# A layer norm, a recurrent gate network and ALiBi attention on eight cores: another order of loads, of the ramp and of the last gate steps

## The chip, the cores and the metric

The kernel runs on the 8 cores of one Trainium2 chip. Each core works on one batch element of its own, and the cores exchange nothing. The metric is the device time of the slowest core in microseconds (us). A profile shows one execution on its slowest core.

## What is computed

For x of 4096 tokens by 1024 features (float32), per batch element:

```
xn = layernorm(x)
s  = attention(xn)      # 16 heads of 64, keys and queries exchanged, ALiBi bias, softmax
g  = silu(net(xn))      # three cycles, below
x  = x + s * g

gf = sigmoid(global_net(mean over tokens of xn))
out = xn
three times:
    tf  = sigmoid(gelu(gelu(gelu(out @ w1 + b1) @ w2 + b2) @ w3 + b3) @ w4 + b4)   # 1024, 512, 256, 1
    out = out + coupling(gf, tf) * twist(out)   # one number per token; twist permutes four quarters of the features
```

## The kernel before

**Engines and queues.** TensorE (PE) does the matmuls, VectorE (DVE) the norms, sums and copies, ScalarE (ACT) GELU, tanh, exp and some copies, GpSimd (POOL) the inverse square roots and all weight DMAs (they cast float32 to bf16), SyncE (SP) the other DMAs. Each engine runs its own list of instructions in order, written out by hand (`pe_program`, `act_program`, `dve_program`, `gp_program`, `sp_program`), and they wait for each other by semaphores. A waiting instruction holds everything behind it on its engine.

**Front.** Tokens come in 32 tiles of 128 (512 KB each), six buffers deep: tile t waits for the norm of tile t - 6. VectorE makes mean and variance (`stats(s)`, two tiles a pair), GpSimd turns a pair's variance into r = (var + eps)^-0.5 and nmr = -mean * r in four steps (L424 to L430), VectorE writes XN = x * r + nmr in bf16 (`norm(s)`, L1083). In VectorE's list `norm(s)` stands behind `stats(s + 1)`. PE transposes a tile (L483), ScalarE copies it into XB (L779), which holds all of xn transposed. Behind every fourth tile PE makes token sums for the global net. From tile 4 on each tile is followed by one item of the list EARLY (30 items, table SPREAD; the last three stand behind tile 31): layer 1 of blocks 0 to 2, 256 tokens each, cycle 1, with their layers 2 and 3. GpSimd issues the seven weight DMAs of both nets once tile 3 has landed (L412 to L418): W1 2048 KB as bf16, W2 1024, W3 256, W4 64, GW1 1024, GW2 256, GW3 64.

**Network.** A block is 256 tokens, 16 blocks in all (E11 to E15 are the last). Layer 1 is linear, so it is computed once for xn (U, `uv_unit(e, 0, i)`) and once for the twisted xn (V, `uv_unit(e, 1, i)`), in four units each; W1N is W1 negated, for the twist's signs. The pre-activations of cycles 2 and 3 are then sums U + c V and a U + b V on VectorE (`pre2`, `pre3`) with factors c, a, b per token that come from the cycle before (`couple1`, `couple2`, `couple3`). A cycle is: 8 GELUs (`gelu_u` or `gelu_pre`), `layer2` (32 matmuls), `gelu2`, `layer3`, `gelu3`, `layer4`, `tanh_z`, a coupling. The loop over p runs cycle 1 of block p, cycle 2 of block p - 2 and cycle 3 of block p - 3 beside each other. P_ORD and Z_ORD number the passes through the shared PSUM banks. `cab` holds what the coupling takes from the global net; no coupling can run before it.

**Gate.** When a block's three cycles are through (`gate_scalars`), its two chunks of 128 tokens are loaded again (XF), scaled on ScalarE (`scale_x`, L858 and L859), twisted and added on VectorE (`add_twist`, L1194 and L1196), passed through tanh (`tanh_y`, L865), multiplied (`gate`, L1203) and stored to g_s in HBM. Below, "chunk 14" and "chunk 15" mean the two chunks of block E14 and of E15.

**Attention.** Heads go in 8 pairs. Each pair needs projections in units of 512 tokens, 4 pieces of matmuls each: K (copied to KT), V (times the ALiBi weights, to VB) and Q (to QT). The class Plan makes the order: `groups` are up to four score blocks of 128 keys by 256 queries, one exp of up to 128 x 1024 each (1024 groups); a `job` is a pair and 256 queries (the first jobs have 14 groups). `build()` goes in rounds r: scores of groups 2r and 2r + 1 ("S"), products with V of groups 2r - 3 and 2r - 2 ("AV"), then pieces of later units ("W") as their due round, `window(u)`, asks. PE's list is P.pe. VectorE's is P.dve: W copies a unit, O copies a job's sums out of PSUM, N divides, multiplies by g, adds x; these are put in by a running estimate of when they are ready. The first n_early = 17 units (K, V and Q0 of the first pair) are made before the exps in banks 0 and 1, later ones in bank 7. SyncE loads g and x for each job (GS, XS, four buffers) and stores its result.

Of the kernel before, what the change touches and what calls it, by code (L numbers as in the profile page):

```python
# [41 lines left out]
E_LAST = NE - 1  # L42

class Plan:

# [99 lines left out]
def build_program():  # L147
# [160 lines left out]
    Z_ORD = []  # L308
    for p in range(1, NE - 1):
        if p - 3 >= 0:  # L310
            P_ORD.append((p - 3, 3))
# [39 lines left out]
    def sp_program():  # L351
        SY.dma_start(out=identb[:], in_=identb_h[:]).then_inc(sConst, 16)
        SY.dma_start(out=biases[:], in_=bias_h[:]).then_inc(sConst, 16)
        for t in range(NT):
# [1107 lines left out]
```

## Time and profile before

| | |
|---|---|
| median of 3 runs | 1543.62 us (1542.3 to 1544.22) |
| the profiled execution, its own time | 1534.47 us |
| its span on the slowest core | 1532.9 us (others 1528.3 to 1532.9) |
| PE busy | 1378.9 us (90%) |
| ACT busy | 1332.8 us (87%) |
| DVE busy | 791.6 us (52%) |
| mean granted TensorE clock | 0.98 of full speed |

The span runs from the first to the last instruction of a core; the profiled execution is 1.57 us longer than it and 9.15 us shorter than the median of the runs. Busy shares are means over stages that are bound by different things, so the stages are to be read one by one. Times in the rows are from the span's start.

### The profile page before, as it was taken

The numbers are of one execution on the slowest core, as the hardware profiler recorded it, in microseconds if no ns is written. First come the engines' busy times: TensorE is split into PE (matmuls) and PEld (weight loads), VectorE is DVE, ScalarE is ACT, GpSimd is POOL, SyncE is SP. The second block draws the span as 40 slices with busy tenths as digits, with TensorE's granted clock in tenths as the row PEclk, the third lists the DMA queues.
The fourth block names the chain that finished last, engine by engine and source line by source line (L and its number), as shares of the span: only waits on it lengthen the run. The fifth ranks groups of instructions, "written<-read, shape, count | busy, mean of one in ns | idle before, by whom it ended". The sixth has DMA issues, their size and how long they took to land.

```text
span 1532.9 us, 49645 instructions; the slowest of 8 cores (1528.3 to 1532.9 us)
## 1 busy us (share of the span) xinstructions
PE 1378.9 (90%) x18394; PEld 940.1 (61%) x18394; DVE 791.6 (52%) x1863; ACT 1332.8 (87%) x2009; POOL 49.9 (3%) x104
## 2 busy tenths in 40 slices
PE   1696799999999995999999999999999999999997
PEld 1585688888888863555755444565554444655554
DVE  2774687887878893222222333333333434434666
ACT  1355698988988874999999999999999999999998
POOL 2331000000000000000000000000000000000000
PEclk9998899999999997999999999999999999999999
DMA  8851013122121116311112112113321212222333
GB/s 177 226 163 42 26 57 111 56 73 94 57 103 65 56 56 152 91 33 33 34 47 57 43 44 64 44 43 64 78 61 54 64 53 57 71 64 73 111 106 113
DMA packets 122391, 115.58 MB, mean 75 GB/s; under 512 B 8368, under 2 KB 106928, under 8 KB 121776
## 3 DMA queue, kind: packets, MB, share of 16 engines
q1 hardware_dynamic: 118848, 101.26, 21.2%
q0 software_dynamic: 3312, 11.14, 4.6%
q8 instruction: 157, 2.57, 0.7%
q14 instruction: 74, 0.61, 0.1%
HBM read 89.96 MB, written 33.55 MB: 81 GB/s over the span
## 4 chain that ended last, share of the span: by engine, by line
PE 77%; DVE 7%; issue 5%; DMA 4%; ACT 4%; DVEq 2%; POOL 0%; SPq 0%; ACTq 0%; POOLq 0%
PE PS L747 20%; PE PS L765 18%; PE PS L513 14%; PE PS L529 11%; PE PS L613 9%; ACT PB L877 3%; DMA XT<-x 3%; PE PS L608 3%; PE PS L541 3%; DVE ACC L1375 3%; DMA XF<-x 1%; DVE SST L1393 1%; PE PS L483 1%; DVE QT L1229 0%; PE PS L554 0%
## 5 line engine op out<-in xcount | busy, mean ns | idle before, releaser
L877 ACT ACTIVATE PB<-PS 128x1024 bf16<-128x1024 f32 (+2 forms) x1088 | 906.8, 1037 | 9.6 <-PE PS L747 8.3
L747 PE MATMUL PS<-QT,KT 64*128 64x256 bf16 x3888 | 373.3, 273 | 39.4 <-ACT PB L877 21.3
L765 PEld LDWEIGHTS PS<-VB,PB 128*128 128x128 bf16 x7776 | 274.8, 97 | 167.6 <-issue 165.9
L765 PE MATMUL PS<-VB,PB 128*128 128x66 bf16 x7776 | 344.7, 194 | 24.8 <-DVE ACC L1375 23.4
L747 PEld LDWEIGHTS PS<-QT,KT 64*128 64x128 bf16 x3888 | 147.1, 94 | 265.8 <-issue 239.7
L513 PE MATMUL PS<-XB,W 128*128 128x256 bf16 x1536 | 207.8, 276 | 0.0
L529 PE MATMUL PS<-H,W 128*128 128x256 bf16 x1536 | 181.9, 276 | 10.4 <-ACT H L802 9.6
L1375 DVE COPY ACC<-PS 128x264 f32<-128x264 f32 x128 | 55.4, 432 | 228.6 <-PE PS L765 228.3
L529 PEld LDWEIGHTS PS<-H,W 128*128 128x128 bf16 x1536 | 150.1, 99 | 32.8 <-issue 14.6
L613 PE MATMUL PS<-XB,WQ 128*128 128x512 bf16 x512 | 154.4, 385 | 10.7 <-DVE VB L1225 7.8
L513 PEld LDWEIGHTS PS<-XB,W 128*128 128x128 bf16 x1536 | 150.2, 99 | 18.5
L820 ACT ACTIVATE H<-PS,biases_s 128x256 bf16<-128x256 f32 x192 | 80.7, 474 | 56.0 <-PE PS L529 54.4
L1393 DVE SCALAR_TENSOR_TENSOR SST<-ACC,den,GS 128x64 f32<-128x64 f32 x512 | 111.7, 280 | 12.5 <-issue 2.6
L1229 DVE CAST QT<-PS 128x512 bf16<-128x512 f32 x64 | 44.2, 691 | 142.7 <-PE PS L613 142.6
L608 PE MATMUL PS<-WKV,XB 128*128 128x128 bf16 x1152 | 83.0, 219 | 1.4 <-DVE KT L1229 1.3
L791 ACT ACTIVATE H<-U,biases_s 128x256 bf16<-128x256 f32 x128 | 59.1, 503 | 27.2 <-DVE U L1097 27.2
L613 PE MATMUL PS<-XB,WKV 128*128 128x512 bf16 x288 | 81.2, 378 | 0.5 <-DVE KT L1229 0.5
L513 PE MATMUL PS<-XB,W1N 128*128 128x256 bf16 x512 | 77.5, 274 | 0.0
L1229 DVE CAST KT<-PS 128x512 bf16<-128x512 f32 x36 | 24.9, 690 | 87.3 <-PE PS L613 87.1
L483 PE MATMUL PS<-identb_s,XN 128*128 128x128 bf16 x256 | 22.9, 244 | 51.3 <-DVE XN L1083 42.0
L608 PEld LDWEIGHTS PS<-WKV,XB 128*128 128x128 bf16 x1152 | 66.1, 97 | 2.3 <-issue 1.8
L802 ACT ACTIVATE H<-PRE,biases_s 128x256 bf16<-128x256 f32 x128 | 61.2, 502 | 4.1 <-DVE PRE L1126 4.1
(98 smaller groups left out, 1177.6 us busy)
## 6 DMA issues: line engine op xcount, KB each, us to landing
XT<-x SPq DMA_DIRECT2D x32, 512.0 KB, 5.4
XF<-x SPq DMA_DIRECT2D x32, 512.0 KB, 5.5
g_s<-TY SPq DMA_DIRECT2D x32, 512.0 KB, 3.0
GS<-g_s SPq DMA_DIRECT2D x128, 128.0 KB, 2.5
XS<-x SPq DMA_DIRECT2D x128, 128.0 KB, 2.4
out<-SST SPq DMA_DIRECT2D x128, 128.0 KB, 1.8
WKV<-wkv POOLq DMA_DIRECT2D x8, 512.0 KB, 7.6
W<-w POOLq DMA_DIRECT2D x1, 2048.0 KB, 17.9
```

Of the source, the lines that this page charges most:

```text
L513: x = TE.matmul(bank[:, q * TE_:(q + 1) * TE_], w, XB[:, src * S + e * TE_:src * S + (e + 1) * TE_], start=(f == 0), stop=(f == NF - 1))
L529: x = TE.matmul(bank[:, q * TE_:(q + 1) * TE_], W2[:, f * 512 + f2 * 128:f * 512 + (f2 + 1) * 128], H1[cyc - 1][:, f * TE_:(f + 1) * TE_], ...
L608: x = TE.matmul(bank[:, piece * 128:(piece + 1) * 128], XB[:, f * S + nt * 128:f * S + (nt + 1) * 128], w[:, f, :], start=(f == 0), stop=( ...
L613: x = TE.matmul(bank, w[:, f, :], XB[:, f * S + c * 512:f * S + (c + 1) * 512], start=(f == 0), stop=(f == NF - 1))
L747: x = TE.matmul(BANK[2 * (g % 3) + b % 2][:, (b // 2) * 256:(b // 2 + 1) * 256], KT[i][hh * 64:(hh + 1) * 64, (nt - KT0[i]) * 128:(nt - KT ...
L765: x = TE.matmul(BANK[6][:, (2 * hh + j) * VW:(2 * hh + j + 1) * VW], PB[g % NPB][:, col_of(b) + j * 128:col_of(b) + (j + 1) * 128], vbv[i] ...
L802: SE.activation(out=H1[cyc - 1][:, f * TE_:(f + 1) * TE_], in_=src[:, q * TE_:(q + 1) * TE_], func=AF.Gelu, bias=b1c[:, f:f + 1]).then_inc ...
L820: k = SE.activation(out=H2[n % 2][:, f * TE_:(f + 1) * TE_], in_=BANK[3 + i][:, q * TE_:(q + 1) * TE_], func=AF.Gelu, bias=b2c[:, f:f + 1])
L877: x = SE.activation(out=dst[:, k, t], in_=src[:, k, t], func=AF.Exp, bias=-MARGIN, scale=1.0 / 32.0)
L1229: VE.tensor_copy(out=dst[:, c0 * 512:(c0 + 1) * 512], in_=bank).then_inc(vU, 1)
L1375: VE.tensor_copy(out=ACC[n % NACC][:], in_=BANK[6][:, 0:4 * VW]).then_inc(vO, 1)
L1393: VE.scalar_tensor_tensor(out=SST[k][:, c0:c0 + 64], in0=acc[:, b, 0:64], scalar=rd[:, b:b + 1], in1=GS[k][:, c0:c0 + 64], op0=AOP.mult, o ...
```

## The change

1. **Front.** W1 leaves first, in two parts (six eighths, two eighths), without waiting for a tile; SyncE holds tile 3 and all behind it until the first part has landed. W2 to W4 are issued behind GpSimd's second pair, the global net's weights behind its seventh. EARLY's items stand behind tiles 2 to 31, one each. VectorE adds eps itself (a drain and a TENSOR_SCALAR of 128 x 2 in `stats`); GpSimd's power takes the variance as it is, and `norm` waits for it alone (XN = (x - mean) * r, the mean from VectorE's own tile). GpSimd still makes nmr, for the gate.
2. **Ramp.** The passes p = 1 to 4 of the loop are written out in another order on PE, ACT and DVE: units of block 3 stand between the cycles of blocks 0 and 1. The loop begins at p = 5.
3. **Into the exps.** Before the exps stand 12 units (eight K, Q0, three V); the V units 3 to 7 follow among the first rounds, one in each of rounds 0 to 4. The gate steps of chunk 14 move in among the exps (scaling before groups 8 and 9, tanh before 14 and 15), those of chunk 15 from groups 2 to 5 to groups 28, 29, 36 and 37. VectorE has them as ("G", 0) to ("G", 3) in P.dve, which now begins with the copies of V3 to V7, then G0, O0, the copy of Q1, G1, N0, Q2, O1, Q3, G2, N1, Q4, G3. SyncE stores chunk 14 and loads chunk 15 behind the first eight loads of GS and XS, and stores chunk 15 behind the second store of a result.

```diff
+NV0 = 3
+GATE_AT = (10, 16, 30, 39)
...
-        first, later = self.pair_units(0), []
-        self.n_early = len(first) - (NC - 1)
-        later += first[self.n_early:]
+        units = self.pair_units(0)
+        first = [u for u in units if u[0] == "K"] + [("Q", 0, 0)] + [u for u in units if u[0] == "V"][:NV0]
+        later = [u for u in units if u not in first]
+        self.n_early = len(first)
...
+        if kind == "V" and i == 0:
+            g = min(g for g in range(self.first[(0, 0)], self.last[(0, 0)] + 1)
+                    if any(nt // 4 == c for _, nt, _ in self.groups[g][2]))
+            return 0, (g + 3) // 2 + 1
...
+        gates = [(through[g], 14, ("G", k)) for k, g in enumerate(GATE_AT)]
         for when, cost, op in urgent:
+            while gates and gates[0][0] < when:
+                free = max(free, gates[0][0]) + gates[0][1]
+                self.dve.append(gates.pop(0)[2])
...
-    SPREAD = [EARLY[k - 4:k - 3] if 4 <= k < NT - 1 else EARLY[NT - 5:] if k == NT - 1 else [] for k in range(NT)]
+    SPREAD = [EARLY[k - 2:k - 1] if k >= 2 else [] for k in range(NT)]
...
         for t in range(NT):
+            if t == 3:
+                SY.wait_ge(sW1[0], 16)
...
-        for e in range(NE):
+        def load_x(e):
...
+        def store_g(e):
...
+        for e in range(NE - 2):
+            load_x(e)
+            store_g(e)
+        load_x(NE - 2)
...
         for n in range(NST):
             load(n)
+        store_g(NE - 2)
+        load_x(NE - 1)
         for n in range(NP * NQ):
             SY.wait_ge(vF, n + 1)
             SY.dma_start(out=rows(out_h, n), in_=slot(SST, n)).then_inc(sSO[n % NST], 16)
+            if n == 1:
+                store_g(NE - 1)
...
-        GP.wait_ge(sX[3], 16)
-        GP.dma_start(out=W1[:], in_=w1_h[:]).then_inc(sW1, 16)
-        GP.dma_start(out=W2[:], in_=w2_h[:]).then_inc(sWF, 16)
...
+        GP.dma_start(out=W1[:, 0:6 * D], in_=w1_h[:, 0:6 * D]).then_inc(sW1[0], 16)
+        GP.dma_start(out=W1[:, 6 * D:], in_=w1_h[:, 6 * D:]).then_inc(sW1[1], 16)
         for s in range(NT // 2):
             GP.wait_ge(vStat, s + 1)
...
-            GP.tensor_scalar(out=r, in0=mv[:, :, 1], scalar1=EPS, scalar2=None, op0=AOP.add).then_inc(gVar, 1)
-            GP.wait_ge(gVar, s + 1)
-            GP.tensor_tensor(out=r, in0=r, in1=minus_half[:], op=AOP.pow).then_inc(gRstd, 1)
+            GP.tensor_tensor(out=r, in0=mv[:, :, 1], in1=minus_half[:], op=AOP.pow).then_inc(gRstd, 1)
...
+            if s == 1:
+                GP.dma_start(out=W2[:], in_=w2_h[:]).then_inc(sWF, 16)
...
+            if s == 6:
+                GP.dma_start(out=GW1[:], in_=gw1_h[:]).then_inc(sGW, 16)
...
-        for p in range(1, NE - 1):
+        layer4(0, 1)
+        uv_unit(3, 0, 0)
+        layer4(1, 1)
+        uv_unit(3, 0, 1)
+        uv_unit(3, 0, 2)
+        layer2(0, 2)
+        layer3(0, 2)
+        layer4(0, 2)
+        layer4(2, 1)
+        layer2(1, 2)
+        layer3(1, 2)
+        layer4(1, 2)
+        layer2(0, 3)
+        uv_unit(3, 0, 3)
+        layer3(0, 3)
+        uv_unit(3, 1, 0)
+        layer4(0, 3)
...
+        layer3(4, 1)
+        for p in range(5, NE - 1):
...
-        project(12)
...
-        project(16)
...
-                    TE.wait_ge(vU, P.uidx[("Q", i, c // 2)] + 1)
+                    TE.wait_ge(vU, max(P.uidx[("Q", i, c // 2)] + 1, P.n_early))
...
+                if (i, c) == (0, 0):
+                    TE.wait_ge(vU, max(P.uidx[("V", 0, nt // 4)] for _, nt, _ in blocks) + 1)
...
-        scale_x(2 * E14)
-        scale_x(2 * E14 + 1)
-        tanh_y(2 * E14)
-        tanh_y(2 * E14 + 1)
         for g in range(NG):
-            if g in (2, 3):
-                scale_x(2 * E_LAST + g - 2)
-            if g in (4, 5):
-                tanh_y(2 * E_LAST + g - 4)
+            if g in (8, 9):
+                scale_x(2 * E14 + g - 8)
+            if g in (14, 15):
+                tanh_y(2 * E14 + g - 14)
+            if g in (28, 29):
+                scale_x(2 * E15 + g - 28)
+            if g in (36, 37):
+                tanh_y(2 * E15 + g - 36)
...
-                x = VE.bn_aggr(mv[:, 2 * j:2 * j + 2], st[:, 12 * j:12 * j + 12])
-            x.then_inc(vStat, 1)
+                VE.bn_aggr(mv[:, 2 * j:2 * j + 2], st[:, 12 * j:12 * j + 12])
+            VE.drain()
+            VE.tensor_scalar(out=mv[:, 1:4:2], in0=mv[:, 1:4:2], scalar1=EPS, scalar2=None,
+                             op0=AOP.add).then_inc(vStat, 1)
...
-            VE.wait_ge(gNmr, s + 1)
+            VE.wait_ge(gRstd, s + 1)
...
+                c0 = 4 * (s % NMV) + 2 * (li % 2)
+                VE.tensor_scalar(out=XN[li % NXN][:], in0=XT[li % NXT][:], scalar1=mvs[:, c0:c0 + 1],
+                                 scalar2=rcol[:, li:li + 1], op0=AOP.subtract, op1=AOP.mult).then_inc(vNorm, 1)
...
+            elif op == ("G", 0):
+                add_twist(2 * E14)
+                add_twist(2 * E14 + 1)
+                gate_scalars(E15)
+            elif op == ("G", 1):
+                gate(2 * E14)
+                gate(2 * E14 + 1)
+            elif op == ("G", 2):
+                add_twist(2 * E15)
+                add_twist(2 * E15 + 1)
+            elif op == ("G", 3):
+                gate(2 * E15)
+                gate(2 * E15 + 1)
```

## Rows read from the trace of the kernel before

**Rows 1.** Stretches: us, busy us of each engine (instructions), granted clock, DMA share, GB/s.
```profile
20.00:45.00 25.00, 4.72 (x64) 4.19 (x64) 9.15 (x18) 5.14 (x5) 4.78 (x11) 1.00 1.01 191
...
141.50:183.10 41.60, 26.22 (x218) 18.64 (x216) 23.94 (x28) 20.44 (x53) 1.18 (x2) 0.75 0.22 58
183.10:210.90 27.80, 27.80 (x267) 24.94 (x265) 22.76 (x36) 24.27 (x56) 0.00 (x0) 1.00 0.22 77
...
580.00:614.00 34.00, 16.48 (x178) 9.86 (x175) 12.10 (x24) 15.41 (x18) 0.00 (x0) 0.70 0.56 150
...
650.00:700.00 50.00, 48.19 (x707) 25.72 (x706) 13.00 (x39) 50.00 (x60) 0.00 (x0) 1.00 0.12 34
```

**Rows 2.** Timeline, 14 to 142 us: start, us, engine, line, operation [idle before, releaser].
```profile
14.75 0.66 POOL L412 DMA_DIRECT2D W<-w  x1 [13.27 <-DMA XT<-x]
...
20.55 1.53 DVE L1083 TENSOR_SCALAR XN<-XT,rcol,nmr 128x1024 bf16<-128x1024 f32 x2 [4.66 <-POOL nmr L430]
...
38.14 0.69 DVE L1068 BATCH_NORM_STATS2 stat<-XT 128x6 f32<-128x512 f32 x1 [11.93 <-DMA XT<-x]
...
45.92 3.62 PE L513 MATMUL PS<-XB,W 128*128 128x256 bf16 x16
...
64.46 1.01 PE L483 MATMUL PS<-identb_s,XN 128*128 128x128 bf16 x8 [3.40 <-ACT XB L779]
...
141.93 0.94 PE L568 MATMUL PS<-gctb,GW 128*128 128x1 bf16 x32
```

**Rows 3.** The page, DMA issues: engine, count, KB each, us to landing.
```profile
W<-w POOLq DMA_DIRECT2D x1, 2048.0 KB, 17.9
```

**Rows 4.** DMA packets of 12 to 14 us (tiles alone) and 20 to 26 us (W1 alone).
```profile
DMA packets 204, 0.74 MB, mean 371 GB/s; under 512 B 23, under 2 KB 23, under 8 KB 204
...
DMA packets 63, 1.03 MB, mean 172 GB/s; under 512 B 0, under 2 KB 0, under 8 KB 0
```

**Rows 5.** Timeline of the ramp, VectorE and TensorE.
```profile
145.79 0.15 DVE L1260 TENSOR_SCALAR cab<-cab 128x1 f32<-128x1 f32 x1
...
172.86 5.56 PE L529 MATMUL PS<-H,W 128*128 128x256 bf16 x28 [2.00 <-ACT H L802]
...
199.08 3.66 PE L513 MATMUL PS<-XB,W 128*128 128x256 bf16 x32
202.57 3.66 PE L529 MATMUL PS<-H,W 128*128 128x256 bf16 x32
...
226.89 3.66 PE L513 MATMUL PS<-XB,W 128*128 128x256 bf16 x32
```

**Rows 6.** The ramp as one stretch, columns as in rows 1.
```profile
145.90:226.90 81.00, 67.44 (x581) 55.77 (x582) 61.09 (x87) 58.19 (x136) 0.86 (x2) 0.89 0.19 56
```

**Rows 7.** Timeline before the exps, TensorE, then ScalarE.
```profile
577.03 9.09 PE L608 MATMUL PS<-WKV,XB 128*128 128x128 bf16 x160
593.25 3.57 PE L613 MATMUL PS<-XB,WQ 128*128 128x512 bf16 x8 [7.13 <-DVE VB L1225]
...
592.20 0.81 ACT L858 ACTIVATE TY<-XF,fin 128x512 f32<-128x512 f32 x1 [1.34 <-DMA XF<-x]
...
598.27 1.28 ACT L877 ACT_TABLE_LOAD   x1 [1.88 <-PE PS L747]
...
606.85 0.81 ACT L858 ACTIVATE TY<-XF,fin 128x512 f32<-128x512 f32 x1 [5.34 <-DMA XF<-x]
...
608.27 1.00 ACT L877 ACTIVATE PB<-PS 128x1024 bf16<-128x1024 f32 x1
...
611.49 1.04 ACT L865 ACTIVATE XF<-TY 128x1024 f32<-128x1024 f32 x1
...
614.29 26.45 ACT L877 ACTIVATE PB<-PS 128x1024 bf16<-128x1024 f32 x31
```

**Rows 8.** Chain that ended last: start, us, what.
```profile
577.11 14.96 DMA XF<-x
...
600.41 6.30 DMA XF<-x
```

More of the change, by code:

```diff
@@ L78, in __init__ @@
         later.sort(key=lambda u: (self.window(u)[1], u[1], "KVQ".index(u[0]), u[2]))
-        self.units = first[:self.n_early] + later
+        self.units = first + later
         self.uidx = {u: r for r, u in enumerate(self.units)}
@@ L263, in build_program @@
     sX = [sem(f"sX{i}") for i in range(NXT)]
-    sW1, sWF, sGW, sWT = sem("sW1"), sem("sWF"), sem("sGW"), sem("sWT")
+    sW1 = [sem(f"sW1{i}") for i in range(2)]
+    sWF, sGW, sWT = sem("sWF"), sem("sGW"), sem("sWT")
     sWKV = [sem(f"sWKV{i}") for i in range(NKV)]
@@ L625, in early_item @@
                 if (e, v, i) == (0, 0, 0):
-                    TE.wait_ge(sW1, 16)
+                    for k in range(2):
+                        TE.wait_ge(sW1[k], 16)
                 if (e, v, i) == (0, 1, 0):
@@ L649, in pe_program @@
         TE.wait_ge(aT, NT)
-        for p in range(1, NE - 1):
+        layer4(0, 1)
[15 more added lines that the diff above has]
+        layer4(0, 3)
+        uv_unit(3, 1, 1)
+        uv_unit(3, 1, 2)
+        layer2(3, 1)
+        uv_unit(3, 1, 3)
+        uv_unit(4, 0, 0)
+        layer3(3, 1)
+        uv_unit(4, 0, 1)
+        layer2(1, 3)
+        layer4(3, 1)
+        layer2(2, 2)
+        layer3(1, 3)
+        uv_unit(4, 0, 2)
+        layer4(1, 3)
+        layer3(2, 2)
+        uv_unit(4, 0, 3)
+        layer4(2, 2)
+        uv_unit(4, 1, 0)
+        uv_unit(4, 1, 1)
+        layer2(4, 1)
+        uv_unit(4, 1, 2)
+        uv_unit(4, 1, 3)
+        layer3(4, 1)
+        for p in range(5, NE - 1):
             A, F, B, C, _ = runs(p)
@@ L760, in pe_program @@
                         TE.wait_ge(gWhl, i + 1)
+                if (i, c) == (0, 0):
+                    TE.wait_ge(vU, max(P.uidx[("V", 0, nt // 4)] for _, nt, _ in blocks) + 1)
+                if P.first[(i, c)] == g:
                     if g > 0:
@@ L1257, in dve_program @@
         VE.wait_ge(aGF, 3)
+        VE.wait_ge(gNmr, NT // 2)
         VE.scalar_tensor_tensor(out=cab[:, 2:3], in0=thg[:], scalar=0.7, in1=arc, op0=AOP.mult, op1=AOP.mult)
@@ L1261, in dve_program @@
         VE.drain()
-        for p in range(1, NE - 1):
+        couple1(0)
+        pre2(0, 0)
+        pre2(0, 1)
+        couple1(1)
+        pre2(1, 0)
+        pre2(1, 1)
+        couple2(0)
+        pre3(0, 0)
+        pre3(0, 1)
+        couple1(2)
+        pre2(2, 0)
+        empty_u(3, 0)
+        empty_u(3, 1)
+        pre2(2, 1)
+        empty_u(3, 2)
+        couple2(1)
+        empty_u(3, 3)
+        pre3_products(1, 0)
+        couple3(0)
+        gate_scalars(0)
+        pre3_sum(1, 0)
+        pre3(1, 1)
+        add_twist(2 * 0)
+        add_twist(2 * 0 + 1)
+        empty_u(4, 0)
+        empty_u(4, 1)
+        gate(2 * 0)
+        gate(2 * 0 + 1)
+        couple1(3)
+        pre2(3, 0)
+        pre2(3, 1)
+        empty_u(4, 2)
+        couple3(1)
+        gate_scalars(1)
+        empty_u(4, 3)
+        couple2(2)
+        pre3(2, 0)
+        pre3(2, 1)
+        for p in range(5, NE - 1):
             A, F, B, C, Dg = runs(p)
```

130 lines of the change are left out of this document (89 added, 41 removed).

## The prediction, made before the result was known

> **What bounds the kernel now.** I read the page first, then a table of stretches, then the timeline of the three places in which TensorE is not full. Four stages follow one another. From 0 to 142 us the input is normalized and transposed, with the first three 256-token blocks of the coupling network put between the tiles; from 142 to 227 us the network's pipeline fills; from 227 us it runs in periods; then come the first projections, and from 614 us the exps of the attention. In a period PE is busy 27.80 of 27.80 us, and from 650 us on ACT is busy 50.00 of 50.00 us [rows 1]: the change touches neither, and a stage shifted as a whole keeps its length. PE idles in the front (4.7 us busy of 20 to 45 us), in the ramp (26.2 of 41.6 us, granted clock 0.75) and before the exps (16.5 of 34 us, clock 0.70) [rows 1]. All the change can give lies there.
>
> **Part 1, the front.** Before, the weights (seven casting DMAs) go out behind the fourth tile, from 14.75 us on and 0.66 us each, and GpSimd's first steps for a norm stand behind them, so that the first norm waits 4.66 us for nmr; the seventh tile, asked for at 22 us, lands among the weights and stops VectorE for 11.93 us until 38.14. The first unit of layer 1 runs at 45.92 us, at half clock (3.62 us), and the transposes of tile 8 at 64.46 us [rows 2]. W1 takes 17.9 us from issue to landing [rows 3]; alone on the engines it moves 172 GB/s (counted in bf16), while tiles alone move 371 GB/s [rows 4].
> After, W1 leaves at about 1.5 us, six eighths of it (1.57 MB) first; SyncE holds tile 3 until they are there. My estimate: 1.57 MB at 172 GB/s is 9.1 us, tiles 0 to 2 (1.57 MB) at 371 are 4.2 us, and the engines start near 4 to 7 us, so tile 3 is asked for at 17 to 20 us (the bound from above is the row of W1: 1.5 + 17.9 = 19.4) and lands some 4 us later. Stats of pair 1 end near 24.5; norm 0 follows at once, since the pow of pair 0 is long done; then stats 2 and norm 1 (4 x 0.69 + 1.5 = 4.2 us [rows 2]) give the first unit at 29 to 30 us, now behind tile 2 instead of tile 4. Tiles 6 and 7 come at about 30, tiles 8 and 9 against W2 to W4 (1.35 MB, 7.8 us of the engines). I put tile 6, whose step now holds the item that tile 8 had, at 45 us against 64.46. Ends: 41 if the tiles don't feel the weights, 55 if they take the 16 us that tile 6 took. The DMAs of W2 to W4 now stand before pair 2 on GpSimd's queue, those of the global net before pair 7; three issues take 2 us, and a pair's result is not needed until a pair later: no cost.
> What follows to the global net took 141.93 - 64.46 = 77.5 us [rows 2]. It holds two transposes more between items (0.9 us), the last step no longer holds three items, and VectorE has a drain and a tiny TENSOR_SCALAR more in each pair: 0.23 us by the nearest pair of rows (the drain and 0.15 us of L1260) [rows 5], 13 pairs, 3.0 us, of which half lies where PE and not VectorE is late. GpSimd's shorter way (pow alone) is worth nothing here, since norm(s) runs behind stats(s+1): only the first norm ever waited for POOL. With up to 1 us for the global net's weights, now loaded in the fifties: 77.5 + 0.9 + 1.5 + 1 = 80.9. The global net starts at 126, **gain 16 us**, ends 6 and 20.
>
> A rule of the Trainium skill bears on this (DMA: Bandwidth & Descriptors, Queues, rings and completion order): each DMA engine goes round robin between its queues, packet by packet. By it the big packets of W1 would slow tiles 0 to 2 as well, against the order that the change wants; the trace agrees as far as tile 6 shows it. By that rule the first unit comes at about 31 instead of 29.5, inside the ends above.
>
> **Part 2, the ramp.** From cab known (145.9) to the first unit of block 5 (226.9) are 81.0 us [rows 5]. Unit pairs and layer 2 start 3.49 us apart, and a period (block 4's to block 5's unit) is 27.81 us [rows 5]. The work of PE between is two periods, 55.6, and one layer 2, a layer 3 and three layers 4 of block 0 and 1, 5.3: 61 us, so 20 us are waits and half clock. The busy times of the stretch are 67.4, 61.1 and 58.2 us (PE, DVE, ACT) [rows 6]: no order ends it under about 65 us with VectorE's drains, and that is the upper end of the gain, 16.
> I walked the new lists by hand with these durations, on the clock of before. Units 3,0,0 to 3,0,2 (5.3 us) run while PE waits for pre2 of block 0, so layer 2 of (0,2) runs at full clock and ends at 156.7. GELUs of (0,2), coupling, pre3 and the GELUs of (0,3) follow; nothing shortens these. Layer 2 of (0,3) ends at 174.8, against 172.86 + 5.56 = 178.4 [rows 5], with 6 us more of the list done. From there PE's list holds 13 units, 4 layers 2, 5 layers 3 and 4 layers 4: 22.8 + 14.0 + 4.4 + 1.0 = 42.2 us, and I find no wait in it, since the list never asks for a block within 5 us of the GELUs that feed it. Block 5 starts at 217.3 instead of 226.9. VectorE's list ends its last pre3 at 215.6 and ACT's its last GELU at 217.9, so all three are level and a late one has no cover; the later start of periods is then the same as before. **Gain 9.5 us**, ends 3 and 13.
>
> **Part 3, the way into the exps.** Before, PE makes five V units in 9.09 us from 577.03 and then waits 7.13 us for VectorE, which stands at the twist of chunk 14, behind ACT and a load of 14.96 us; exps 0 and 1 run from 599.6, exp 2 waits for the next load (5.34 us), and only from exp 5 at 614.29 do they run end to end, 31 in 26.45 us, 0.853 each [rows 7, 8]. Counted back, that is a start at 614.29 - 5 x 0.853 = 610.0 with all gate work done.
> After, Q0 takes the ninth place, three V units stay, and scores start when V2 is copied. PE has layer 4 of the last block done and V2 begun at 577.0, so + 1.8 + 0.7 for the copy: 579.9; the table load of 1.28 us [rows 7] puts exp 0 at 582. Rounds 0 to 4 (two groups each) carry a whole V unit: 9.09 / 5 = 1.8 us, beside 2 x 0.58 for scores and products (48.2 us of PE for 60 exps between 650 and 700, less half a piece each [rows 1]): 2.9 us, where ACT needs 1.7. Five rounds end at 594. ACT meanwhile has the two scalings of chunk 14 before exps 8 and 9, 1.42 us each (606.85 to 608.27), the second of which waits for its load until 592.2, as before; exp 10 starts at 594.5. From there ACT sets the pace. Left are two tanh (1.04 us long, 0.95 apart by the 0.1 that scalings overlap: 0.81 long, 0.71 apart) and chunk 15's two scalings and two tanh: 1.9 + 4.7 = 6.6 us. Counted back: 594.5 - 8.5 + 6.6 = 592.6, **gain 17.4 us**, ends 8 and 20.
> What is queued behind the moved steps: VectorE's two gates of chunk 14 stand behind O0 and Q1's copy and run at about 602 to 604, SyncE's store of chunk 14 stands behind the eight loads of GS and XS (over by 590) and goes at 604, the load of chunk 15 at 606. At 6.30 us it lands at 612 [rows 8], when exp 28 is due (594.5 + 1.9 + 18 x 0.853 = 611.8): no slack. The store of chunk 15 stands behind the second store of out and ahead of the loads for job 5, which are needed 40 us later; GpSimd's weight columns and jobs 14 and 15 that wait for it are hundreds of us away.
>
> A rule of the Trainium skill speaks against this part (ScalarE: Activation LUTs, Table sets: the hidden batching unit): activations should be batched by table set. Eight returns to another set, with a load each way as in the row, would cost 16 x 1.28 = 20 us and eat the gain. In the trace chunk 15's scaling and tanh already stand between exps without a load, so I give it nothing; the page's own list has tanh in the set of exp.
>
> **Sum.** 16 + 9.5 + 17.4 = 42.9 us. The profiled execution took 1534.47 us and would take 1491.6; the runs' median is 1543.62, 9.15 above it, and I keep that distance: 1500.7, given as 1501.
>
> **Rivals.** *A, the tiles starve:* each tile takes 16 us while any weight is loading; the item of tile 8 comes at 55. For it speaks the row of 11.93 us, against it that before 4.6 MB of weights stood ahead and now 1.35. Front 6: 1511. *B, chunk 15's load is long:* 14.96 us like chunk 14's instead of 6.30 holds exp 28 by 8.7 us: 1509. For it: the eight loads of GS and XS; against: they and the WQ loads are over by then. *C, PE is the bound among the exps:* it is 96% busy there (48.2 of 50 us [rows 1]), and the five V units (9.1 us) then come on top: 1510. *D, slower:* the hand order of the ramp crosses a chain. From cab to layer 2 of (0,3) are 27.1 us for two cycles of one block [rows 5], 13.5 a cycle; an engine that stands at the head of its list for a result of a later cycle costs that each time. The ramp's gain and four such waits, 9.5 + 54, give 1564; it decides from the fourth on (42.9 / 13.5 = 3.2). My walk found none. *E, no change:* the waits come back elsewhere: A (10), B (8.7), C (9.1) and a ramp without gain (9.5) together leave 5.6, and one wait more of that size leaves 1543.
>
> **Chances.** Forecast 0.61, A 0.12, B 0.11, C 0.08, better than the ends' middle by over 10 us 0.04, D 0.02, E 0.02. About 0.2% (3 us) is what a measurement of this kernel can tell from no change. Faster 0.96, same 0.02, slower 0.02. The range takes in A, B and C alone, and from the ends of the three parts (42.9 + 13, - 17) 1488 to 1518.
>
> **What would show it.** Right: first layer 1 unit near 30 us and the global net near 126; block 5's first unit near 201.4; exp 0 near 556.5 (582 less 25.5) and exp 10 near 569; ACT full from there; PE's clock near 1.00 in the ramp. Wrong: VectorE waiting over 5 us for tiles behind pair 3; ACT idle at L858 among the exps; a wait of PE over 3 us in the ramp; exps apart by more than 0.853 after the fifth round.

## The result, and the profile after

The changed kernel takes 1518.2 us (three executions from 1517.24 to 1518.20) beside 1543.92 for the kernel before: a ratio of 0.9833 (95% interval 0.9814 to 0.9853), 25.7 us faster. The forecast was 1501 with a range up to 1518. The direction was right, the size was not. The profiled execution took 1518.16 us (executions in which cores of a die ran some 40 us or more longer, at a mean clock below 0.95, are left out everywhere). The spans and mean granted clocks of its cores:

```profile
core 0: 1504.7 us, clock 0.989
core 1: 1502.2 us, clock 0.990
core 2: 1502.0 us, clock 0.987
core 3: 1504.4 us, clock 0.989
core 4: 1514.5 us, clock 0.982
core 5: 1511.6 us, clock 0.981
core 6: 1514.1 us, clock 0.981
core 7: 1516.6 us, clock 0.979
```

Before, all eight stood between 1528.3 and 1532.9 at 0.979 to 0.981. Now they fall into two groups: four gained 27 to 28 us, four only 14 to 21, at a lower clock. Core 7 sets the time; core 3 shows what the change does without that.

**The front** (timeline of core 7; start, us, engine, line, operation, idle before), to be laid beside [rows 2]:

```profile
1.89 0.67 POOL L431 DMA_DIRECT2D W<-w  x1 [0.42 <-issue]
...
19.84 0.69 DVE L1203 BATCH_NORM_STATS2 stat<-XT 128x6 f32<-128x512 f32 x1 [11.19 <-DMA XT<-x]
...
27.57 1.53 DVE L1222 TENSOR_SCALAR XN<-XT,mvs,rcol 128x1024 bf16<-128x1024 f32 x2
...
33.80 3.62 PE L533 MATMUL PS<-XB,W 128*128 128x256 bf16 x16
...
45.48 0.69 DVE L1203 BATCH_NORM_STATS2 stat<-XT 128x6 f32<-128x512 f32 x1 [3.85 <-DMA XT<-x]
...
50.94 1.01 PE L503 MATMUL PS<-identb_s,XN 128*128 128x128 bf16 x8 [4.75 <-DVE XN L1222]
...
135.99 0.94 PE L588 MATMUL PS<-gctb,GW 128*128 128x1 bf16 x32
```

VectorE gets tile 1 only at 19.84 us, after 11.19 us of waiting beside W1; it gets the ninth tile (tile 8) at 45.48, after 3.85 us more of waiting; the first unit of layer 1 runs at 33.80 (before 45.92), tile 6 is transposed at 50.94, and the global net starts at 135.99 (before 141.93).

**The network** (stretches: busy us of PE, PEld, DVE, ACT, POOL with the number of instructions, then granted clock, DMA share, GB/s; first core 7, then cores 2 and 3), to be laid beside [rows 1]:

```profile
core 7: us, PE busy (x) PEld busy (x) DVE busy (x) ACT busy (x) POOL busy (x), PEclk, DMA share, GB/s
141.50:183.10 41.60, 34.98 (x274) 27.45 (x272) 35.02 (x47) 28.70 (x69) 0.00 (x0) 0.84 0.24 52
218.00:221.00 3.00, 3.00 (x25) 2.49 (x23) 2.16 (x3) 1.96 (x4) 0.00 (x0) 0.81 0.00 0
300.00:400.00 100.00, 100.00 (x924) 88.58 (x922) 78.66 (x118) 83.53 (x190) 0.00 (x0) 0.97 0.27 85
650.00:700.00 50.00, 48.25 (x712) 25.91 (x709) 12.22 (x34) 49.91 (x61) 0.00 (x0) 1.00 0.11 31
...
core 2: us, PE busy (x) PEld busy (x) DVE busy (x) ACT busy (x) POOL busy (x), PEclk, DMA share, GB/s
141.50:183.10 41.60, 34.96 (x283) 28.02 (x281) 34.86 (x49) 30.60 (x74) 0.00 (x0) 0.88 0.11 31
...
core 3: us, PE busy (x) PEld busy (x) DVE busy (x) ACT busy (x) POOL busy (x), PEclk, DMA share, GB/s
141.50:183.10 41.60, 34.23 (x299) 27.92 (x297) 35.56 (x49) 31.61 (x76) 0.00 (x0) 0.96 0.22 57
300.00:400.00 100.00, 100.00 (x955) 89.73 (x954) 80.42 (x129) 87.47 (x200) 0.00 (x0) 1.00 0.27 83
```

The start of the ramp is fuller (35.0 us of PE in 41.6, before 26.2). Its clocks of 0.84, 0.88 and 0.96 there are the half clock alone, which core 7 shows for 12.9 of these 41.6 us, core 2 for 10.2 and core 3 for 3.4. In the periods PE is busy without a gap on cores 3 and 7, yet core 7 does 924 matmuls in 100 us where core 3 does 955. The difference is in stretches of some 5 us, from 183 us on and about one in each period, in which the granted clock is neither of the two levels of the kernel before (1.00 and 0.50 of 2.4 GHz) but 0.81. In the profile of the kernel before no core shows that value.

**The exps** (timeline of core 3):

```profile
564.74 1.28 ACT L935 ACT_TABLE_LOAD   x1 [2.88 <-PE PS L802]
566.04 3.77 ACT L935 ACTIVATE PB<-PS 128x1024 bf16<-128x1024 f32 x4
570.32 1.94 ACT L935 ACTIVATE PB<-PS 128x1024 bf16<-128x1024 f32 x2 [0.52 <-PE PS L802]
573.39 1.94 ACT L935 ACTIVATE PB<-PS 128x1024 bf16<-128x1024 f32 x2 [1.12 <-PE PS L802]
...
576.47 1.11 PE L628 MATMUL PS<-WKV,XB 128*128 128x128 bf16 x17 [1.09 <-issue]
...
578.06 1.02 ACT L935 ACTIVATE PB<-PS 128x1024 bf16<-128x1024 f32 x1 [1.33 <-PE PS L802]
...
580.39 4.59 ACT L935 ACTIVATE PB<-PS 128x1024 bf16<-128x1024 f32 x6
...
599.26 0.96 ACT L916 ACTIVATE TY<-XF,fin 128x512 f32<-128x512 f32 x1
```

Rounds are 3.07 us apart (570.32 to 573.39), the scaling of chunk 15 finds its load landed (599.26, no wait), and no second table load follows the first.

### The profile page after: what moved, and what is told of

Read it like the earlier page. It is cut to its first block, busy times and chain, and to the rows that moved or that the text cites. A ratio compares the mean times of both kernels' runs of the same rounds, so it can differ in the third digit from the quotient of the medians.

```text
span 1516.6 us, 49662 instructions; the slowest of 8 cores (1502.0 to 1516.6 us)
## 1 busy us (share of the span) xinstructions
PE 1386.6 (91%) x18394; PEld 946.6 (62%) x18394; DVE 795.5 (52%) x1879; ACT 1333.5 (88%) x2009; POOL 38.7 (3%) x89
## 4 chain that ended last, share of the span: by engine, by line
PE 79%; DVE 6%; issue 5%; ACT 4%; DMA 4%; DVEq 1%; ACTq 0%; POOL 0%; SPq 0%; POOLq 0%
PE PS L802 20%; PE PS L823 18%; PE PS L533 14%; PE PS L549 11%; PE PS L633 9%; PE PS L628 4%; ACT PB L935 3%; DMA XT<-x 3%; PE PS L561 3%; DVE ACC L1551 2%; DMA W<-w 1%; DVE SST L1569 1%; PE PS L574 1%; PE PS L503 0%; DVE QT L1368 0%
## 5 line engine op out<-in xcount | busy, mean ns | idle before, releaser
L533 PE MATMUL PS<-XB,W 128*128 128x256 bf16 x1536 | 215.8, 284 | 0.0
L533 PEld LDWEIGHTS PS<-XB,W 128*128 128x128 bf16 x1536 | 153.9, 102 | 22.3
L633 PE MATMUL PS<-XB,WQ 128*128 128x512 bf16 x512 | 151.2, 378 | 4.3 <-DVE QT L1368 2.2
L1364 DVE TENSOR_TENSOR VB<-PS,WT 128x512 bf16<-128x512 f32 x36 | 24.9, 691 | 84.4 <-PE PS L628 83.7
```

The lines of the kernel that those rows point to most:

```text
L533: x = TE.matmul(bank[:, q * TE_:(q + 1) * TE_], w, XB[:, src * S + e * TE_:src * S + (e + 1) * TE_], start=(f == 0), stop=(f == NF - 1))
L633: x = TE.matmul(bank, w[:, f, :], XB[:, f * S + c * 512:f * S + (c + 1) * 512], start=(f == 0), stop=(f == NF - 1))
```

## The experiments

The experiments ran in five groups (e to i), each on a chip of its own, here called 2 to 6; the result's chip is called 1, and the records don't tell which it is. The kernel before ran beside each group, at a median of 1536.65 to 1538.82 us. To compare parts, I cut every profiled execution at three stations that lie on the path: the global net's first matmul, block 5's first unit, the first exp. The values are means over the cores that show no 0.81, unless cores are named (us):

| kernel | chip | global net | to block 5 | to exp 0 | to the end | ratio of times, 95% interval |
|---|---|---|---|---|---|---|
| before | 1 | 139.8 | 85.2 | 373.3 | 932.7 | |
| changed, cores 0 to 3 | 1 | 135.0 | 77.0 | 354.8 | 936.5 | |
| changed, cores 4 to 7 | 1 | 136.0 | 78.3 | 363.7 | 936.2 | 0.9833 (0.9814 to 0.9853) |
| e1 changed, cores 6 and 7 | 2 | 134.2 | 77.5 | 354.8 | 935.9 | 0.9971 (0.9945 to 0.9996) |
| e2 part 1 alone | 2 | 136.2 | 86.2 | 373.2 | 932.4 | 0.9960 (0.9937 to 0.9984) |
| e3 part 2 alone | 2 | 139.6 | 78.6 | 372.9 | 932.3 | 0.9942 (0.9904 to 0.998) |
| e4 part 3 alone | 2 | 140.9 | 85.7 | 354.8 | 935.7 | 0.9883 (0.9835 to 0.9931) |
| f1 parts 1 and 3 | 3 | 135.7 | 86.0 | 354.8 | 935.3 | 0.9872 (0.9858 to 0.9886) |
| f2 softened ramp | 3 | 136.5 | 82.3 | 354.8 | 936.2 | 0.9846 (0.983 to 0.9861) |
| f3 f1, GW late | 3 | 133.6 | 86.0 | 354.8 | 935.8 | 0.9858 (0.9844 to 0.9872) |
| f4 f1, eps on POOL | 3 | 132.9 | 85.4 | 354.8 | 936.5 | 0.9859 (0.9845 to 0.9873) |
| g1 changed | 4 | 135.9 | 77.2 | 354.8 | 936.3 | 0.9816 (0.9803 to 0.9829) |
| g2 softened ramp | 4 | 136.2 | 82.4 | 354.8 | 935.7 | 0.9852 (0.9839 to 0.9865) |
| g3 two of three units | 4 | 136.0 | 77.8 | 354.8 | 935.9 | 0.9822 (0.9809 to 0.9834) |
| g4 g2, eps and GW | 4 | 130.2 | 82.6 | 354.8 | 935.5 | 0.9813 (0.98 to 0.9825) |
| h1 changed, eps and GW | 5 | 130.6 | 77.1 | 354.8 | 935.5 | 0.9788 (0.9775 to 0.9801) |
| h2 h1, W1 later | 5 | 135.1 | 77.3 | 354.8 | 935.7 | 0.9804 (0.9791 to 0.9817) |
| h3 h1, W2 later | 5 | 128.2 | 78.0 | 354.8 | 935.9 | none given |
| h4 as g4 | 5 | 132.1 | 82.5 | 354.8 | 935.7 | 0.9829 (0.9814 to 0.9843) |
| i1 as h3 | 6 | 129.1 | 77.2 | 354.8 | 934.9 | 0.9769 (0.9755 to 0.9783) |
| i2 i1, two of three units | 6 | 129.1 | 77.3 | 354.8 | 936.0 | 0.9768 (0.9754 to 0.9782) |

In one execution a core's global net lies up to 9 us from another's, and its mean over the cores is 130.2 in g4 and 132.1 in h4, which are the same kernel, so below 2 us the ratios decide. The ratio of e3 stands for its four executions without 0.81 (1528.48 to 1530.77 us); its other seven took 1552.03 to 1554.13 us, more than the kernel before.

### Which part gives what (e1 to e4)

e1 is the changed kernel as it is. e2, e3 and e4 are the kernel before with one of the three parts of the diff; to part 1 belongs one line of the change that the excerpt of its diff leaves out, so that the gate may still use nmr:

```diff
         VE.wait_ge(aGF, 3)
+        VE.wait_ge(gNmr, NT // 2)
```

> The changed kernel once more, beside the kernel before. Its profile gave 28.0 us less than before on core 3 (1532.4 to 1504.4) and 16.3 less on core 7 (1532.9 to 1516.6), where a period of the network is 28.6 us long instead of 27.8 and the granted clock is 0.93 to 0.97 in it. Theory C (the chip's clock): the lower clock of one die is there in timed executions of the kernel before as well, so the ratio stays near 0.983 and the gain near 26 us. Theory P (the plan): the change itself draws the clock down, since TensorE pauses less; then before shows both dies level in every run and the changed kernel never does.

> Part 1 alone (order of the weight DMAs, items from tile 2 on, eps on VectorE, power alone on GpSimd). Theory A (the parts add, each as its stage shows in the trace): global net at about 135 instead of 141.6, 6 to 7 us faster. Rival B (the front's gain depends on what follows it, since the old ramp starts slower behind a busier front): under 4 us or over 10.

> Part 2 alone (passes 1 to 4 in the new order). Theory A: block 5 starts 8 to 9 us sooner, 8 to 9 us faster. Rival B: under 5 us, if the ramp lives on the front's new tail.

> Part 3 alone (12 units ahead of the exps, gate of the last two blocks among them). Theory A: 13 us faster, with exps 0 to 9 about 3.1 us a round. Rival B (DMA traffic at that point decides): the same trace but another length of the loads, gain under 10 or over 16.

By the stages, part 1 gives 4 to 5 us at the global net (of which e2 loses 1 again in the ramp), part 2 gives 7 to 8, part 3 gives 18.5 - 3.0 = 15.5: together some 28, what cores 0 to 3 of the result show. By the ratios the parts are 6, 9 and 18 us, with intervals of 4 to 7 us either way that take in the values of the stages. That is near theory A for e2 and e3; e4 gives more than the 13 us expected. But e1 took 1534.63 us (median), nearly the time of before: the cores of before are level in all but one execution and those of the changed kernel in none, as theory P has it. Its spans and clocks, then stretches of core 5 and core 7:

```profile
core 0: 1530.5 us, clock 0.969
...
core 5: 1532.0 us, clock 0.969
core 6: 1504.5 us, clock 0.988
core 7: 1500.3 us, clock 0.990
...
core 5: us, PE busy (x) PEld busy (x) DVE busy (x) ACT busy (x) POOL busy (x), PEclk, DMA share, GB/s
...
200.00:300.00 100.00, 100.00 (x793) 83.02 (x792) 68.86 (x105) 73.23 (x164) 0.00 (x0) 0.81 0.21 69
...
320.00:420.00 100.00, 100.00 (x952) 89.71 (x951) 80.85 (x120) 86.05 (x196) 0.00 (x0) 1.00 0.28 86
...
core 7: us, PE busy (x) PEld busy (x) DVE busy (x) ACT busy (x) POOL busy (x), PEclk, DMA share, GB/s
200.00:300.00 100.00, 100.00 (x946) 89.68 (x945) 82.47 (x122) 86.44 (x193) 0.00 (x0) 1.00 0.20 72
```

Six cores run at 0.81 from about 148 us on, a few us into the ramp, to about 310 us, broken only by the half clock of the ramp's waits. Core 5 then does 793 matmuls where core 7 does 946, and ends some 30 us later. It comes by pairs of neighbouring cores. With the whole change all 12 otherwise undisturbed executions had one to three such pairs (mean clock near 0.967), with the ramp alone 7 of 11, with part 1 alone none of 11, with part 3 alone none of 4, with the kernel before 1 of 25. So on this chip the new order of the ramp makes it common, though it can come without it.

### Does the filled wait at the ramp's start draw it (f1, f2, g1 to g3, h4, i2)

f1 is parts 1 and 3 with the ramp of before. f2 and g2 are the whole change with three units of PE moved:

```diff
         layer4(0, 1)
-        uv_unit(3, 0, 0)
         layer4(1, 1)
-        uv_unit(3, 0, 1)
-        uv_unit(3, 0, 2)
         layer2(0, 2)
...
         layer4(1, 2)
+        uv_unit(3, 0, 0)
+        uv_unit(3, 0, 1)
+        uv_unit(3, 0, 2)
         layer2(0, 3)
```

In g3 only `uv_unit(3, 0, 2)` is moved so; g1 is the changed kernel again.

> Parts 1 and 3 of the change, with the ramp's order of before. Theory P (the denser ramp is what draws the granted clock of 0.81): no stretch of 0.81 on any core, all eight cores within 0.5% of one another, and the gain is the sum of the two parts alone, 4.8 + 15.5 = 20 us: ratio 0.987 (0.985 to 0.989), faster than the whole change on the same kind of chip (0.9971). Theory F (anything that shortens the stages ahead of the network draws it, the front as well): pairs of cores with 0.81 again, 25 to 30 us longer, ratio 0.995 or above.

> The whole change, but the three units of block 3 that filled PE's wait ahead of layer 2 of (0,2) stand behind layer 4 of (1,2). Theory H1 (it is the filling of that wait, without a pause of PE at the start of the ramp, that starts the long stretch of 0.81): none of it here; the cores lose at most 3 us of fill against the undisturbed cores of the whole change (1500 to 1504 us), so 1504 to 1507 and a ratio near 0.981. Theory H2 (the ramp as a whole is too dense, wherever its units stand): stretches of 0.81 on some cores as before, 1530 us on them, ratio 0.995 to 0.999.

> The whole change once more, beside its variants on one chip, since the runs with and without the granted clock of 0.81 so far were on different chips. Theory P (the ramp's order draws it, on any chip): some pairs of cores have stretches of 0.81 in the network stage, a mean clock of 0.97 to 0.982 and 1512 to 1534 us, the others 0.988 and 1500 to 1505 us; the slowest core sets 1518 to 1535. Theory C (only some chips do it, whatever the ramp): either all of this call's kernels show it, or none, and then the whole is at 1505 to 1508 and a ratio near 0.981.

> As before (the three units behind layer 4 of (1,2)), now on the same chip as the whole change. Theory H1 (filling PE's wait at the ramp's start draws the 0.81): no 0.81 where the whole change shows it, all cores 1507 to 1512 us. Theory C: the same cores show it as in the whole change's run. Where neither shows it, soft is 5 us slower than the whole change: 82.4 us from the global net to block 5 against 76.4.

> Two of the three units of block 3 stay in PE's wait ahead of layer 2 of (0,2), the third moves behind layer 4 of (1,2), so PE pauses there for some 1.8 us. Theory H1 as a matter of degree: between the whole change and soft, block 5 at 78 to 81 us behind the global net, and 0.81 on fewer cores than in the whole change, or none. Theory H1 as a matter of any pause: none of 0.81. Theory C: as the whole change.

f1 has the sum of its two parts by the stages (its ratio of 0.9872 is 19.7 us, forecast 20), without 0.81. f2 has none either, and it looked like a confirmation, but it ran on another chip than e1. g1, on a third, shows that the chip decides too: no core of the changed kernel has 0.81 there, and it takes 1508.25 us, ratio 0.9816. With nothing to avoid, softening costs 5.2 us of the ramp (82.4 against 77.2). TensorE's timeline of core 4, first in g1, then in g2, shows why:

```profile
146.35 0.60 PE L549 MATMUL PS<-H,W 128*128 128x256 bf16 x4
147.10 4.09 PE L549 MATMUL PS<-H,W 128*128 128x256 bf16 x28 [0.15 <-ACT H L860]
...
212.31 3.66 PE L533 MATMUL PS<-XB,W 128*128 128x256 bf16 x32
```

```profile
146.04 1.57 PE L549 MATMUL PS<-H,W 128*128 128x256 bf16 x4 [3.21 <-ACT H L860]
148.48 6.23 PE L549 MATMUL PS<-H,W 128*128 128x256 bf16 x28 [0.87 <-ACT H L860]
...
168.28 6.80 PE L533 MATMUL PS<-XB,W 128*128 128x256 bf16 x48
...
220.29 3.66 PE L533 MATMUL PS<-XB,W 128*128 128x256 bf16 x32
```

Where PE waited 3.21 us the layer 2 behind it runs mostly at half clock, 6.23 us for 28 matmuls, where after the filled wait it takes 4.09, and the three units now stand where PE has no wait for them to fill (6.80 us from 168.28 on). g3 with two of three units in the wait loses 0.6 us by the stages and 0.9 by the ratios, whose intervals overlap.

Groups h and i put the ramps side by side once more. h4 is g4's kernel, to be compared with h1, which has the full ramp; i2 is i1 with g3's edit.

> The first kernel with the softened ramp, on the same chip. Where no core shows 0.81: 5 us slower than the first kernel, 1508. Where the chip grants 0.81 to the dense ramp and theory H1 holds: all cores 1500 to 1506 us, no 0.81, and 15 to 25 us faster than the first kernel. Where H2 holds (any shorter ramp draws it): 0.81 on pairs of cores here too.

> The same with one of the three units of block 3 behind layer 4 of (1,2). Where neither shows 0.81: 0.7 us slower (0.6 us as the whole change and its variant on one chip). Where the first shows it: theory H1 as a matter of any pause, no pair of cores at 0.967 to 0.973 in any execution; as a matter of degree, fewer than in the first.

By the ratios h4 is 6.3 us slower than h1 (0.9829 against 0.9788), and i2 is level with i1. On chip 5 the kernels with the full ramp (h1 to h3) had a pair at a mean clock near 0.97 and some 22 us longer in 3 of 13 executions, the softened one in none of 3; on chip 6 neither kernel had any. These executions were not the profiled ones, so that they had 0.81 stretches is inferred from their clocks. Three against none is too few to show that the filled wait, and not the ramp as a whole, is what matters: that stays open. Shown is only that e3's edit makes the long stretches common on chip 2.

### Why the front gave 4 to 6 us of 16 (f3, f4, g4, h1 to h3, i1)

f3 issues the global net's weights later; f4 gives eps back to GpSimd but lets norm wait for the power alone, as the change does:

```diff
-            if s == 6:
+            if s == 11:
```

```diff
-            GP.tensor_tensor(out=r, in0=mv[:, :, 1], in1=minus_half[:], op=AOP.pow).then_inc(gRstd, 1)
+            GP.tensor_scalar(out=r, in0=mv[:, :, 1], scalar1=EPS, scalar2=None, op0=AOP.add).then_inc(gVar, 1)
+            GP.wait_ge(gVar, s + 1)
+            GP.tensor_tensor(out=r, in0=r, in1=minus_half[:], op=AOP.pow).then_inc(gRstd, 1)
...
-            VE.drain()
-            VE.tensor_scalar(out=mv[:, 1:4:2], in0=mv[:, 1:4:2], scalar1=EPS, scalar2=None,
-                             op0=AOP.add).then_inc(vStat, 1)
+            x.then_inc(vStat, 1)
```

> Parts 1 and 3, the three loads of the global net's weights issued behind GpSimd's pair 11 instead of 6. Theory G (these 1.3 MB starve the tiles near 62 to 80 us): VectorE's waits for tiles there (1.97 and 0.95 us) go, and the global net starts 1.5 to 3 us earlier than in the kernel with parts 1 and 3. Theory S (tiles are late from the first weights on, and stay so at the pace of VectorE and PE): under 0.7 us; or later, if the weights come too late for the global net (landing behind 125 us).

> Parts 1 and 3, eps added on GpSimd as before (one more GpSimd step ahead of the power), VectorE without its drain and TENSOR_SCALAR in stats; norm still waits for the power alone. Theory V (VectorE's addition is on the path of the front: 0.35 us a pair over 13 to 15 pairs): the global net starts 2 to 5 us earlier. Theory N (VectorE has slack, or the longer GpSimd step makes the norm wait instead): within 1 us, with a wait of VectorE for rcol at the first pair of 0.5 us or more.

> Soft, with eps added on GpSimd as in the kernel before (norm still waits for the power alone) and the loads of the global net's weights behind pair 11. Alone beside parts 1 and 3 these gave 2.8 and 2.1 us at the global net (mean of the cores). Theory A (they add up, since both free VectorE's and the tiles' path): the global net at 131 to 132.5 us, 1508 us in all, the fastest of the four. Theory B (both take away the same wait): 2.5 to 3 us in all, 1510.

> The whole change, with eps added on GpSimd again (norm waits for the power alone) and the loads of the global net's weights behind pair 11. On the softened ramp the two took 6 us off the start of the global net (136.2 to 130.2, mean of the cores) and 5.4 us off the time. Theory A (the front's gain goes through whole): 1508.3 less 5.5, about 1503, ratio 0.978, on a chip without 0.81, the fastest of all. Theory P (the dense ramp, on a chip that grants 0.81): pairs of cores 20 to 30 us longer, slower than the kernel with the softened ramp of this call.

Each gives some 2 us by the ratios, whose intervals overlap with f1's (2.1 for f3 and 2.8 for f4 at the global net), and together 6.0 on the softened ramp (0.9852 to 0.9813, 136.2 to 130.2) and 4.3 on the full one (g1's 0.9816 to h1's 0.9788, on two chips; 5.3 at the global net): they add up, within the scatter. So eps on VectorE is a loss of 2 to 3 us as made: the drain and the extra operation lie on VectorE's path (in the changed kernel norm starts 0.46 us behind the start of the aggregate, in h1 0.20), while what they spare GpSimd is hidden, since norm(s) stands behind stats(s + 1).

h2 and h3 take away the two collisions by themselves:

```diff
+        GP.wait_ge(sX[2], 16)
         GP.dma_start(out=W1[:, 0:6 * D], in_=w1_h[:, 0:6 * D]).then_inc(sW1[0], 16)
```

```diff
-            if s == 1:
+            if s == 3:
                 GP.dma_start(out=W2[:], in_=w2_h[:]).then_inc(sWF, 16)
```

> As the one before, but W1 is issued only when tile 2 has landed. Theory R (W1 and the tiles share the DMA engines packet by packet, and so tile 1 comes at 20 instead of 9 us): tiles 1 and 2 are read by 10 to 12 us, W1's first part lands 9 to 12 us after its issue near 11, tile 3 follows at 24 to 26; the first unit of layer 1 at 28 to 30 instead of 34 us, and the global net 3 to 5 us earlier. Theory S (the same bytes have to pass either way): tile 3 comes as much later as tiles 1 and 2 come earlier, and the global net moves by less than 1 us either way, or 2 us later, since the engines stand idle while W1's descriptors are made.

> As the first, but W2 to W4 behind GpSimd's pair 3 instead of 1. Theory A (rival A of the prediction: a tile takes 16 us while these weights load, which stops VectorE for 4.6 us near 45 us): the wait moves to tiles 10 and 11, which have more tiles ahead of them; the global net starts within 1.5 us of the first kernel's. Theory B (the early tiles are the ones that matter, since PE has nothing else then): the global net 3 us earlier. Theory D (W2 comes too late for the first layer 2): PE waits for W2 near 60 us, global net later.

> The kernel with W2 to W4 behind pair 3 once more: 1500 to 1502 us where no core shows 0.81, ratio 0.976 to 0.978; theory B (the early tiles matter) holds if the ratio is below 0.9778, the interval's middle of the kernel with W2 to W4 behind pair 1 less 0.1%. Theory P: on a chip that grants 0.81, some executions with a pair of cores at a mean clock of 0.967 to 0.973 and 1518 to 1527 us.

In h2 (core 3, timeline, and W1's row of its DMA issues) tile 1 does come at 9.49 us, and W1's first part, alone on the engines, lands 11.8 us after its issue instead of 16.4 in h1:

```profile
9.49 0.69 DVE L1206 BATCH_NORM_STATS2 stat<-XT 128x6 f32<-128x512 f32 x1 [1.08 <-DMA XT<-x]
...
11.22 0.66 POOL L432 DMA_DIRECT2D W<-w  x1 [9.75 <-DMA XT<-x]
...
29.43 0.69 DVE L1206 BATCH_NORM_STATS2 stat<-XT 128x6 f32<-128x512 f32 x1 [17.15 <-DMA XT<-x]
...
36.84 2.90 PE L536 MATMUL PS<-XB,W 128*128 128x256 bf16 x16
```

```profile
W<-w POOLq DMA_DIRECT2D x1, 1536.0 KB, 11.8
```

But tile 3, which waits for it, comes at 29.43 us (25.87 in h1), and norm 0 stands behind its stats: the first unit is 3.6 us later (33.27 in h1), the global net 4.5 by the mean of the cores and 2.5 by the ratios (0.9804 against 0.9788, overlapping). Theory R has the early tiles and W1's landing right and what follows wrong; theory S is right in kind, but the global net moves by more than its 2 us. So sharing was not the loss. That a first norm which does not wait for tile 3 would help is my reading of the list; no run tests it. h3 and i1 keep VectorE fed where it had nothing else. VectorE's longest wait for a tile behind the first three, core 3, in h1 and then in i1:

```profile
45.58 0.69 DVE L1205 BATCH_NORM_STATS2 stat<-XT 128x6 f32<-128x512 f32 x1 [4.45 <-DMA XT<-x]
```

```profile
52.82 0.69 DVE L1205 BATCH_NORM_STATS2 stat<-XT 128x6 f32<-128x512 f32 x1 [3.33 <-DMA XT<-x]
```

The wait moves four tiles on and shrinks, and the time falls: h3's two executions without a pair at the lower clock took 1499.97 and 1502.01 us beside 1502.45 to 1506.86 of h1's four, and i1, on another chip, has a ratio of 0.9769. Its middle is below the bound set for theory B, but the intervals of h1 and i1 overlap, so 1 to 3 us is likely and not certain. i1 and i2, 1503.23 and 1502.77 us beside 1538.82, are the fastest kernels with a ratio of their own: some 36 us below before, where the change alone gave 25.7 and 28.4.

## Why the prediction was wrong in size

The forecast had the profiled execution's span at 1532.9 - 42.9 = 1490.0 us; core 7 took 1516.6. The stations split the 26.6 us that are missing, up to rounding:

| stage, core 7 | forecast | measured | missing |
|---|---|---|---|
| global net starts | 126 | 135.99 | 10.0 |
| to block 5 (201.4 - 126) | 75.4 | 80.5 | 5.1 |
| to exp 0 (582 - 226.9) | 355.1 | 364.2 | 9.1 |
| to the end | 933.5 | 936.0 | 2.5 |

(933.5 is 1532.9 - 17.4 less 582.) The 9.15 us between the profiled execution and the median, which I kept, were gone after the change: the other executions agree with the profiled one. That is why the miss against 1501 is 17 us and not 26.6: a gap that I could not explain, and that no run explains, hid 9 us of it by luck.

**The term "gain 16 us" of the front failed.** Three of its steps were short. The first unit was put at 29.5 and came at 33.80: I gave tiles 0 to 2 their 4.2 us at 371 GB/s, as if they left before W1; they shared with it, tile 1 came at 19.84, and 17.4 us from issue to landing were near the bound from [rows 3]. Here the trace had spoken, and so had the Trainium skill (DMA: Bandwidth & Descriptors, Queues, rings and completion order), whose round robin between queues I priced at 1.5 us: it agrees, as tile 1's 19.8 us beside W1 and 9.5 in h2 without it show, but h2 also shows that without the sharing the front is no faster. The step to tile 6 was 17.1 us instead of 15.5, and from tile 6 to the global net 85.0 instead of 80.9, where VectorE's addition of eps cost 2 to 2.8 us (I took 1.5) and the global net's weights about 2 (I took 1). Rival A was half right: tile 8, asked for at 32.9 us beside W2 to W4, is read only at 45.48, but VectorE waits 3.85 us for it, where it waited 11.93 for tile 6 before. Tile 6, whose norm stands behind the stats of tiles 8 and 9, is transposed at 50.9, between the 45 of the forecast and the 55 of the rival. That GpSimd's shorter way is worth nothing here agrees with f4, which has a step more on GpSimd and is no slower. The nearest rows gave 0.23 us for drain and addition; they took 0.26 in the pair above.

**The ramp was right, without the clock.** 9.5 us forecast, 8.2 measured as the mean of cores 0 to 3, which have no 0.81 (85.2 to 77.0), and the walk missed no chain: rival D is out. These four differ: core 2 needs 79.0 us, the others 76.3 to 76.5, and core 2 alone has 17.0 us of half clock in it, where the others have 6.8. That layer 2 of (0,2) would run at full clock because the wait ahead of it is filled was right too (4.09 against 6.23 us above).

**The clock was no term of the sum at all.** The sign was "near 1.00 in the ramp"; the row has 0.84 (before 0.75), all of it half clock. Core 7 has 17.0 us of half clock in the ramp as core 2 has, and with it core 2 is 2.6 us behind cores 0, 1 and 3 (79.0 against 76.4). From 183.3 us on come the stretches of 0.81: they leave core 7 another 1.5 us behind core 2 in the ramp (80.5 against 79.0) and cost 9.4 us up to the exps (364.2 against 354.8 on core 3, which runs the same list). On chip 1 these 11 us are more than the ramp gave, on chip 2 the long stretch eats nearly all of the change. The trace of before did not show such a value, but it did show PE busy without a gap in the periods on all cores at once (28.00 of 28.00 us from 230 to 258), and a change that makes this state begin earlier and more abruptly deserved a rival. The Trainium skill has one (TensorE: Matmul & The Clock Gate, Seeing it yourself): a limiter that sets a whole die to 13/16 of full clock once three of its cores run dense matmuls. The level agrees (0.81). The rest differs: here it takes pairs of cores, for 5 us in a period or for some 160 us once, on two of six chips' profiles, and the same dense load runs at 1.00 on the others.

**The exps were right but for 2 to 3 us.** Exp 0 came 354.8 us behind block 5 on all cores at full clock, forecast 355.1. From there I had 933.5 and measured 934.9 to 936.5: rounds took 3.07 us for 2.9, and on core 3 PE paused 1.09 us between two halves of a V unit, so that exp 10 came 14.4 us (core 7) to 15.3 us (core 3) behind exp 0, forecast 12.5. Gain 15.5 of 17.4. Rival B is out (chunk 15's scaling waits for nothing), C is out (ACT 49.91 of 50 us from 650 on). On the table loads the row decides: one load at exp 0 and none at the scalings and tanhs among the exps. The 16 loads that I held against this part don't follow from the Trainium skill (ScalarE: Activation LUTs, Table sets: the hidden batching unit): its list has tanh in the set of exp and the identity, which the scalings are, in every set, and the trace agrees.

## What to carry to other kernels

Cut profiles before and after at a few stations on the path and price each stage over all cores: sums that failed by 26.6 us fell apart into four terms at once. An operation put on the engine that often sets a stage's pace costs time however small (from aggregate to norm 0.46 us a pair with drain and addition, 0.20 without, 2 to 3 us of the kernel), while what it spares an engine that nobody waits for is worth nothing. A large load that the first matmuls need may go ahead of the first tiles (h2, which held it back, was 2.5 to 4.5 us slower); later loads are better held back by a few pairs (h3 and i1, likely 1 to 3 us). Look at the first consumer's place in its queue before blaming the transfer. Before a difference between cores is put down to one level of the clock, list the stretches of each level on both.

## What the runs showed of the hardware

A granted clock of 0.81, between the two levels, in 5 us stretches in each period (cores 4 to 7 of the result) or in one from about 148 to 310 us (e1). It costs some 9 to 11 us in the first form and some 30 in the second, comes by pairs of neighbouring cores, differs from chip to chip (none in any profile of chips 3 to 6), and was made common by a denser start of the network on chip 2. What sets it off was not found. The half clock of the ramp comes in other lengths on cores with the same list: 6.8 us in all on cores 0, 1 and 3 of the result, 17.0 on core 2, which needs 79.0 us to block 5 where they need 76.3 to 76.5.
